# Keeping the first weights of all sixteen experts on chip, and picking a tile's weight there by a register address

## The chip, the cores and the metric

The kernel runs on one core of a Trainium2 chip. The core has a matrix engine (TensorE, PE in the rows, with a queue of its own for loading weights, PEld), a vector engine (VectorE, DVE), a scalar engine (ScalarE, ACT), GpSimd (POOL) and SyncE (SP), which here only issues DMAs. Each engine runs its own program in order, and they wait for one another by semaphores. SBUF is the memory on chip, PSUM (the `bank`s) the one that TensorE writes. The metric is the device time of one execution in microseconds (us); the number that counts is the median of three runs.

## The reference, cut to what matters

```python
patches = X.reshape(B, C, 8, 28, 8, 28).transpose(0, 2, 4, 1, 3, 5).reshape(B, 64, 2352)
h = concat([cls, einsum('bpi,hi->bph', patches, W) + b]) * pos_embed      # 128 images, 65 tokens, 128 wide
h = h + attention(layernorm(h))                                           # sliding window
x = layernorm(h); z = layer_norm(x, ln_in_g, ln_in_b)
gate = softmax((z @ router_w + router_b) / 0.7)
vals, idx = top_k(gate, 2)                                                # 2 of 16 experts per token
eh = silu(einsum('bsd,edh->ebsh', z, ew1) + eb1)                          # ew1: 16 x 128 x 512
ey = einsum('ebsh,ehd->ebsd', eh, ew2) + eb2                              # ew2: 16 x 512 x 128
mix = sum over the token's two experts of vals * ey
moe = mix + 0.25 * (silu(z @ sw1 + sb1) @ sw2 + sb2)
out = h + x + moe + silu(layer_norm(moe, ff_ln_g, ff_ln_b) @ ff_w1 + ff_b1) @ ff_w2 + ff_b2
```

Everything is float32.

## The kernel before

It is written engine by engine: each engine has one hand-written program, the order of its work is the order of that text, and semaphores carry the waits.

**Stage 1** takes the 128 images in 16 groups of 8 (512 tokens), forms the patch products, attention and the gate, and scatters each token's row twice by GpSimd into `z_rows` in DRAM, where each expert has a section of its own. The images lie in two buffers, the halves of `region`, each `XCOLS` = 14336 columns. The patch weights `wp` and the re-laid pieces `xf` and `xlast` are tensors of their own. The shared expert (`sh_up`, `sh_down`) runs for twelve of seventeen groups in the last group's gaps and behind it.

**Stage 2** is 80 expert tiles of 256 rows: the first 16 are experts 0 to 15, a tile each, the other 64 are handed out by a table that VectorE computes (`ejc`: a tile's expert, `rowj`: its first row). Four tiles are written out, then loops run over four tiles in a turn. For tile j:

- SP reads `rowj` and `ejc` into registers and issues the loads of the rows (`zin`), of `ew1` (L506) and of `ew2` (L508), each into one of four buffers. The `ew2` load waits until tile j-4 has left TensorE (`down_done`).
- TensorE in step j runs the transposes of the rows of tile j+1 (`t_in`, L1615), the first layer of tile j (`up`, L1626) and the second of tile j-1 (`down`, L1637), in this order.
- ScalarE takes the transposed rows from PSUM (L788) and applies silu to `up`'s four blocks (L798).
- VectorE in step j runs `split_rows(j+1)` (L1274, L1275, L1279), `split_w1(j+2)` (L1223, L1225) and `rows_out(j-1)` (L1265, L1268). The first layer's operands are taken apart into a high and a low part in a format that TensorE multiplies in one pass. So `split_w1` makes a cast of the weight (L1223) and a subtraction (L1225), into one of two buffers that `up` of two tiles before must have left. `rows_out` reads the tile's expert into a register (L1259) and adds the bias row, whose address comes from that register, to `down`'s result.
- GpSimd scatters the result to `y_tok` (L916).

In every fourth tile SP also loads residual rows (L542), to which VectorE adds a bias (`fb2_rows`, L1305).

Between stage 1 and the loop SP zeroes the tails of the experts' sections: L412 loads four numbers at a time into registers, L419 issues the writes. Then it loads the weights of stage 3 (L534), two groups of `ht` (L475) and enters the loop (L541).

**Stage 3** gathers each token's two rows, mixes, normalises and runs the last two layers, bound by TensorE.

The buffers of stages 2 and 3 lie over the image buffers in `region`, in an order made by `carve`. Constants that the diff uses: `E` = 16 experts, `W` = 512 columns of one expert's first weight, `FIRST` = 4 tiles whose weights are loaded ahead of time, `GROUPS` = 16, `EXPERT_TILES` = 80, `EARLY` = 12.

Of the kernel before, what the change touches and what calls it, by code (L numbers as in the profile page):

```python
# [68 lines left out]
FILL, EARLY = 7, 12  # L69
SP_TAILS = 12  # L70
# [42 lines left out]
def build(nc, consts, x, tok_w, tok_b, cls_tok, pos, w_c, ln_g, ln_b, r_w, r_b, ew1, eb1, ew2, eb2,  # L113
          sw1, sb1, sw2, sb2, f_g, f_b, fw1, fb1, fw2, fb2, out):
    with ExitStack() as ctx:
# [30 lines left out]
        wp = sb("wp", [P, MAIN, D])  # L146
# [13 lines left out]
        region = sb("region", [P, 2 * XCOLS])  # L160
# [7 lines left out]
        def carve(n):  # L168
            carved[0] += n
            assert carved[0] <= 2 * XCOLS  # L170
            return region[:, carved[0] - n:carved[0]]
# [9 lines left out]
        eh_at = carved[0]  # L181
        ehT = [carve(EC * EROWS).rearrange("p (c r) -> p c r", c=EC) for _ in range(2)]
        zin = [carve(EH * ZW).rearrange("p (h d) -> p h d", h=EH) for _ in range(4)]
        h2T = [carve(EROWS) for _ in range(2)]
        yout = [carve(EH * D).rearrange("p (h d) -> p h d", h=EH) for _ in range(2)]
        fw1_t = carve(DH)
        fw2_t = carve(EC * D).rearrange("p (c d) -> p c d", c=EC)
        r_at = carved[0]
        r_res = carve(TILES * D)
        HT_LOW = (XCOLS - r_at) // GTOK  # L190
        sh_res = carve(TILES * D)


        carved[0] = shared_with_stage3
# [4 lines left out]
        assert carved[0] <= eh_at  # L199
        carved[0] = eh_at  # L200
        gat = [carve(GT * TOPK * D).rearrange("p (t k d) -> p t k d", t=GT, k=TOPK) for _ in range(2)]
        assert 2 * GT * TOPK * D <= 2 * EC * EROWS + 4 * EH * ZW + 2 * EROWS + 2 * EH * D
# [6 lines left out]
        xf = sb("xf", [P, QUADS * 4 * HTOK])  # L209
        xquad = [xf[:, u * 4 * HTOK:(u + 1) * 4 * HTOK].rearrange("p (q t j) -> p q t j", q=2, j=2) for u in range(QUADS)]  # L210
        xlast = sb("xlast", [P, HTOK])
        eb2_rows = xf[:, 0:E * D]
        shs = [xf[:, E * D + u * SC * GTOK:E * D + (u + 1) * SC * GTOK].rearrange("p (c r) -> p c r", c=SC) for u in range(2)]
# [117 lines left out]
        w1_loaded = [sem(f"w1_loaded{u}") for u in range(4)]  # L331
# [94 lines left out]
        def _(sp):  # L426
# [67 lines left out]
            for i in range(HT_LOW, EARLY):  # L494
                load_ht(i)
# [445 lines left out]
        def _(dve):  # L941
# [354 lines left out]
            for j in range(4):  # L1296
                step2(j, j)
# [437 lines left out]
```

## Time and profile before

| | |
|---|---|
| runs | 907.56, 907.61, 908.23 us; median 907.61 us |
| profiled execution, from its first to its last instruction | 972.0 us |
| instructions in it | 22164 |
| busy of that span | TensorE 92%, VectorE 70%, ScalarE 62%, GpSimd 45% |
| read from and written to DRAM | 150.5 MB and 36.0 MB |
| stage 2, first to last `down` | 521.8 to 829.2 us |

The rows below come from that one execution. A time of a row counts from the start of its span. The span is longer than the median of the runs, which were made without a profile. A row of a group of instructions says how often, how long in all and in the mean, and how long the engine stood idle just before them, by what ended that. The end of a product on TensorE is modelled; starts are better to go by.

### The profile page before, as it was taken

To read this page: it belongs to the slowest core of one execution; us is meant where nothing else is said; L and a number is where in the kernel's file an instruction comes from. 1 tells how busy PE (TensorE), PEld (TensorE's weight loads), DVE (VectorE), ACT (ScalarE), POOL (GpSimd) and SP (SyncE) were. 2 spreads that over 40 slices of the span, in tenths; PEclk is the share of its full clock that TensorE was granted. 3 is DMA by queue.
4 is the path that set the end of the run, shared out by engine and by line. 5 is a ranking of instruction groups with operands and counts; after the bars stand their busy time and mean duration, and the time that the engine had idled before them with its cause. 6 is when DMAs were issued, how large, how long until landed. Compare 5 with 4: busy or idle time off the path is not lost. (4 is left out here: it accounts for less than half of the span.)

```text
span 972.0 us, 22164 instructions
## 1 busy us (share of the span) xinstructions
PE 896.2 (92%) x5920; PEld 801.2 (82%) x5920; DVE 676.2 (70%) x2244; ACT 599.5 (62%) x1064; POOL 438.8 (45%) x374
## 2 busy tenths in 40 slices
PE   2999999989999999999889999999999899789999
PEld 2788888778878888888779889898999899679888
DVE  8377877757877887787556666666676675488884
ACT  3567666656666666777645565555555565477766
POOL 6012554425555545554451445455555464334342
PEclk9999999979999999999879999999999999989999
DMA  9999999977788888767137687777778675334432
GB/s 225 224 221 225 242 247 240 237 205 210 213 228 218 214 216 219 194 216 213 50 105 215 196 227 218 214 219 228 216 224 236 184 221 166 107 82 115 107 103 57
DMA packets 194299, 186.96 MB, mean 192 GB/s; under 512 B 16797, under 2 KB 168698, under 8 KB 194010
## 3 DMA queue, kind: packets, MB, share of 16 engines
q1 hardware_dynamic: 183168, 166.24, 65.2%
q0 software_dynamic: 9376, 19.42, 6.1%
q10 hardware_dynamic: 1722, 0.93, 0.5%
q8 instruction: 12, 0.20, 0.1%
q14 instruction: 21, 0.17, 0.1%
HBM read 150.48 MB, written 36.04 MB: 192 GB/s over the span
## 5 line engine op out<-in xcount | busy, mean ns | idle before, releaser
L1435 PE MATMUL bank<-xf,wp 128*128 128x256 f32 x1280 | 314.0, 394 | 8.4 <-ACT xf L632 5.4
L1435 PEld LDWEIGHTS bank<-xf,wp 128*128 128x128 f32 x1280 | 237.7, 192 | 51.6 <-issue 7.4
L916 POOL DMA_INDIRECT y_tok<-region,dsti x160 | 162.9, 1018 | 164.9 <-DVE region L1268 119.0
L874 POOL TENSOR_TENSOR rstd<-var,neghalf 128x4 f32<-128x4 f32 (+2 forms) x51 | 80.6, 1580 | 287.9 <-DVE var L1030 156.4
L632 ACT ACTIVATE xf<-region 128x1024 f32<-128x1024 f32 x160 | 174.0, 1137 | 18.3 <-DVE region L947 18.3
L890 POOL DMA_INDIRECT z_rows<-z,posg x130 | 157.3, 1210 | 52.5 <-issue 52.2
L798 ACT ACTIVATE region<-bank,cols 128x256 f32<-128x256 f32 x320 | 132.3, 476 | 55.2 <-PE bank L1626 37.2
L1637 PE MATMUL bank<-region 128*128 128x128 f32 x1280 | 156.8, 275 | 1.1 <-DVE region L1268 1.0
L1637 PEld LDWEIGHTS bank<-region 128*128 128x128 f32 x1280 | 150.4, 192 | 1.7 <-issue 1.5
L1626 PE MATMUL bank<-parts 128*128 128x256 f32 x960 | 136.6, 290 | 14.2 <-DVE parts L1279 8.8
L1626 PEld LDWEIGHTS bank<-parts 128*128 128x128 f32 x960 | 119.6, 190 | 25.7 <-issue 19.0
L947 DVE COPY region<-region 32x1792 f32<-32x1792 f32 x96 | 104.8, 1092 | 50.3 <-ACT hT L652 28.9
L788 ACT ACTIVATE region<-bank,cols 128x256 f32<-128x256 f32 x80 | 45.4, 567 | 81.0 <-PE bank L1615 46.5
L1223 DVE CAST parts<-region 128x512 fp32r<-128x512 f32 x80 | 35.4, 443 | 70.9 <-DMA region<-in_L_ffn_ew 56.7
L1684 PE MATMUL bank<-region 128*128 128x128 f32 x520 | 61.7, 277 | 0.0
L1684 PEld LDWEIGHTS bank<-region 128*128 128x128 f32 x520 | 59.4, 192 | 0.9 <-ACT region L819 0.5
L1225 DVE TENSOR_TENSOR parts<-region,parts 128x512 fp32r<-128x512 f32 x80 | 55.6, 694 | 2.8
L1329 DVE SCALAR_TENSOR_TENSOR region<-region,w_all 128x128 f32<-128x128 f32 x130 | 50.3, 446 | 7.6 <-issue 5.3
L1665 PE MATMUL bank<-parts,wparts 128*128 128x512 f32 (+1 forms) x204 | 51.5, 403 | 3.4 <-DVE parts L1368 3.4
L1665 PEld LDWEIGHTS bank<-parts,wparts 128*128 128x128 f32 x204 | 37.5, 195 | 12.0 <-issue 3.6
L834 ACT ACTIVATE region<-region,nmr,rstd 128x128 f32<-128x128 f32 x65 | 26.9, 484 | 30.3 <-DVE nmr L1363 30.3
L819 ACT ACTIVATE region<-bank,cols 128x512 f32<-128x512 f32 (+1 forms) x68 | 40.6, 657 | 3.0 <-PE bank L1665 3.0
(183 smaller groups left out, 1232.3 us busy)
## 6 DMA issues: line engine op xcount, KB each, us to landing
region<-in_x SPq DMA_DIRECT2D x384, 196.0 KB
region<-in_L_ffn_ew SPq DMA_DIRECT2D x160, 256.0 KB
region<-z_rows SPq DMA_DIRECT2D x80, 130.0 KB
region<-y_tok SPq DMA_DIRECT2D x16, 512.0 KB, 3.6
ht_dram<-hT SPq DMA_DIRECT2D x16, 256.0 KB
r_dram<-rr SPq DMA_DIRECT2D x16, 256.0 KB
region<-ht_dram SPq DMA_DIRECT2D x16, 256.0 KB, 5.5
region<-r_dram SPq DMA_DIRECT2D x16, 256.0 KB
```

The source lines that it names most:

```text
L632: ins = act.activation(xquad[i].rearrange("p q t j -> p t q j"), src[:, :, 4 * i:4 * i + 4].rearrange("p t (q j) -> p t q j", j=2), ACT.Copy)
L798: act.activation(ehT[n % 2][:, c], bank[1 + c][:, 0:EROWS], ACT.Silu, bias=bias[c])\
L874: pool.tensor_tensor(dst, var, neghalf[:, 0:var.shape[1]], ALU.pow).then_inc(ready, 1)
L890: pool.indirect_dma_start(z_rows, bass.IndirectOffsetOnAxis(posg[k][:, n:n + 1], 0), z[k][:, t], None).then_inc(z_free[k], 16)
L916: pool.indirect_dma_start(y_tok, bass.IndirectOffsetOnAxis(dsti[n % 2][:, i:i + 1], 0), yout[n % 2][:, i], None).then_inc(y_free[n % 2], 16)
L947: dve.tensor_copy(dst, src).then_inc(block_moved, 1)
L1225: dve.tensor_tensor(w1l[n % 2], w1b[n % 4], w1h[n % 2], ALU.subtract).then_inc(w1l_ready, 1)
L1435: ins = pe.matmul(out_cols, wp[:, s], cols_in, start=s == 0, stop=s == MAIN - 1)
L1626: ins = pe.matmul(bank[1 + c][:, 0:EROWS], w[n % 2][:, c * P:(c + 1) * P], v[n % 2], start=i == 0, stop=i == len(terms) - 1)
L1637: ins = pe.matmul(bank[5 + n % 2][:, i * P:(i + 1) * P], ehT[n % 2][:, c, i * P:(i + 1) * P], w2b[n % 4][:, c], start=c == 0, stop=c == EC ...
L1665: ins = pe.matmul(dst, w[:, c * P:(c + 1) * P], v[:, 0:nt * P], start=i == 0, stop=i == len(terms) - 1)
L1684: ins = pe.matmul(bank[FFD_BANK[k]][:, t * P:(t + 1) * P], ffs[:, c, t * P:(t + 1) * P], fw2_t[:, c], start=c == 0 and t == 0, stop=c == E ...
```

## The change

The first weights of all 16 experts get one place each in a buffer `w1all` of 16 x 512 columns and are loaded once: four of them early in the last groups of stage 1 as before, four more (up to `W1_LOW` = 8) somewhat later, and experts 8 to 15 after the tails are zeroed, since their place is part of the second image buffer and of what follows it. In stage 2 SP loads only rows and second weights. VectorE's cast and subtraction read `w1all` at an address from a register. For that it loads the experts of seven tiles at once at the head of every four (`experts`, `four`), for the splits of tiles j+2 to j+5 and the bias rows of tiles j-1 to j+2; `rows_out` has no load of its own any more. The buffers are laid out anew in one larger `region`, which takes in what were `wp`, `xf` and `xlast`; `fw1_t` and `fw2_t` become tensors of their own. The first four `ew2` loads are issued later, behind group 14's stores.

```diff
-        region = sb("region", [P, 2 * XCOLS])
+        XF, XL, WP = QUADS * 4 * HTOK, HTOK, MAIN * D
+        ARENA = 2 * XCOLS + XF + XL + WP
+        region = sb("region", [P, ARENA])
...
+        r_res = carve(TILES * D)
         assert carved[0] <= XCOLS
-        shared_with_stage3 = carved[0]
-        w1b = [carve(W) for _ in range(4)]
+        w1_at = carved[0]
+        w1all = carve(E * W)
+        W1_LOW = (XCOLS - w1_at) // W
...
-            for i in range(HT_LOW):
+            def load_w1(e, done):
+
+                sp.dma_start(w1all[:, e * W:(e + 1) * W], ew1[e]).then_inc(done, 16)
+
+            for i in range(FIRST_HT):
                 load_ht(i)
-            for j in range(FIRST):
-                sp.dma_start(w1b[j], ew1[j]).then_inc(w1_loaded[j], 16)
-                sp.dma_start(w2b[j], ew2[j].rearrange("(c p) d -> p c d", p=P)).then_inc(w2_loaded[j], 16)
+            for e in range(FIRST):
+                load_w1(e, w1_loaded[e])
             one(stores, GROUPS - 3)
...
+            for i in range(FIRST_HT, EARLY):
+                load_ht(i)
+            for e in range(FIRST, W1_LOW):
+                load_w1(e, w1_low)
+            one(stores, GROUPS - 2)
             sp.wait_ge(xact_ready, units_before(GROUPS, 0))
-            for i in range(HT_LOW, EARLY):
-                load_ht(i)
-            one(stores, GROUPS - 2)
+            for j in range(4):
+                sp.dma_start(w2b[j], ew2[j].rearrange("(c p) d -> p c d", p=P)).then_inc(w2_loaded[j], 16)
...
                 ex = sp.value_load(ejc[0:1, bass.ds(j, 1)], min_val=0, max_val=E - 1)
-                sp.wait_ge(w1l_ready, j - 3)
-                sp.dma_start(w1b[n % 4], ew1[bass.ds(ex, 1)].rearrange("o d h -> d (o h)")).then_inc(w1_loaded[n % 4], 16)
                 sp.wait_ge(down_done, j - 3)
...
             zero_tails(sp, FIRST, SP_TAILS)
+            for e in range(W1_LOW, E):
+                load_w1(e, w1_high)
...
-            def split_w1(j, n, h):
+            def experts(j, n):
+
+                return nc.values_load_multi_w_load_instructions(ejc[0:1, bass.ds(j, n)], engines=[dve.engine],
+                                                                min_val=0, max_val=E - 1)[1]
+
+            def split_w1(j, n, ex):
 
                 dve.wait_ge(up_done, j * EC - EC) if n > 1 else None
-                dve.wait_ge(w1_loaded[n % 4], h * 16 + 16)
-                dve.tensor_copy(w1h[n % 2], w1b[n % 4]).then_inc(w1h_ready, 1)
+                w1 = w1all[:, bass.ds(ex * W, W)]
+                dve.tensor_copy(w1h[n % 2], w1).then_inc(w1h_ready, 1)
                 dve.wait_ge(w1h_ready, j + 1)
-                dve.tensor_tensor(w1l[n % 2], w1b[n % 4], w1h[n % 2], ALU.subtract).then_inc(w1l_ready, 1)
+                dve.tensor_tensor(w1l[n % 2], w1, w1h[n % 2], ALU.subtract).then_inc(w1l_ready, 1)
...
-            def rows_out(j, n, h_):
-
-                ex = dve.value_load(ejc[0:1, bass.ds(j, 1)], min_val=0, max_val=E - 1)
+            def rows_out(j, n, h_, ex):
+
...
+            def four(j, n, q=0, after=None):
+
+                ex = experts(j - 1, 7)
+                for m in range(4):
+                    step2(j + m, n + m, q, ex[m + 3], ex[m])
+                    if after and m == 0:
+                        after()
...
+            dve.wait_ge(w1_loaded[3], 16)
+            step2(1, 1, 0, 3, 0)
+            dve.wait_ge(w1_low, 16 * (W1_LOW - FIRST))
+            step2(2, 2, 0, 4, 1)
+            step2(3, 3, 0, 5, 2)
+            dve.wait_ge(w1_high, 16 * (E - W1_LOW))
             dve.wait_ge(w3_loaded, 48)
...
             with dve.Fori(1, 1 + GROUPS) as i:
-                for n in range(4):
-                    step2(i * 4 + n, 4 + n, i - 1)
-                    if n == 0:
-                        fb2_rows(i - 1)
+                four(i * 4, 4, i - 1, lambda: fb2_rows(i - 1))
```

In SP's program at the passage to stage 2, the rows of before run from the last tail (L419) over the weights of stage 3 (`ffn_ff_w`), two `ht` loads and the loop's head to the residual load (`r_dram`):

```order
L419 DMA z_rows<-zeros 128x260
L534 DMA region<-in_L_ffn_ff_w 128x512
L534 DMA region<-in_L_ffn_ff_w 128x4x128
L534 DMA fbq<-in_L_ffn_ff_b 128x128
L475 DMA region<-ht_dram 128x512 x2
L541 UNCONDITIONAL_BRANCH
```

The same place after:

```order
L421 DMA z_rows<-zeros 128x260
L486 DMA region<-in_L_ffn_ew 128x512 x8
L543 DMA fw_t<-in_L_ffn_ff_w 128x512
L543 DMA fw_t<-in_L_ffn_ff_w 128x4x128
L543 DMA fbq<-in_L_ffn_ff_b 128x128
L477 DMA region<-ht_dram 128x512 x2
L550 UNCONDITIONAL_BRANCH
```

Eight loads of first weights now stand ahead of the stage-3 weights and of everything that the loop issues.

In VectorE's program at the head of its stage-2 loop, before (ISA are register and wait instructions; CAST is L1223 on the weight and L1274 on the rows):

```order
L1274 CAST parts<-region 128x256
L1275 ISA
L1275 SCALAR_TENSOR_TENSOR dstf<-region,ejb 128x2
L1279 TENSOR_TENSOR parts<-region,parts 128x256
L1221 ISA
L1222 ISA
L1223 CAST parts<-region 128x512
L1224 REGISTER_ALU
L1225 TENSOR_TENSOR parts<-region,parts 128x512
L1259 ISA
L1259 TENSOR_LOAD ejc
L1259 ISA x2
```

And after:

```order
L1230 TENSOR_LOAD ejc
L1230 ISA x14
L1286 ISA
L1287 REGISTER_ALU
L1288 CAST parts<-region 128x256
L1289 ISA
L1289 SCALAR_TENSOR_TENSOR dstf<-region,ejb 128x2
L1293 TENSOR_TENSOR parts<-region,parts 128x256
L1235 ISA
L1237 ISA
L1237 COPY parts<-region 128x512
L1238 REGISTER_ALU
```

The register load, with two instructions for each of seven numbers, moved from the middle of each tile to the head of four, ahead of `split_rows`, and the wait for the weight's load (L1222) is gone. The weight's cast stands as COPY because its source's address is not fixed in the program.

## Rows read from the trace of the kernel before

**Rows 1.** Table by stretches: start:end, length, busy time by engine, clock, DMA share, GB/s.

```profile
0.00:23.00 23.00, 4.71 (x22) 4.58 (x23) 19.21 (x29) 7.27 (x12) 16.37 (x16) 0.97 0.93 225
...
540.00:820.00 280.00, 262.64 (x2157) 249.17 (x2156) 181.34 (x519) 160.20 (x378) 145.62 (x144) 1.00 0.76 217
...
sum 972.00, PE 896.20 PEld 801.21 DVE 676.20 ACT 599.48 POOL 438.79; mean PE 149.37 PEld 133.54 DVE 112.70 ACT 99.91 POOL 73.13
```

**Rows 2.** TensorE in order of time at stage 2's start: start, length, line, operation.

```profile
525.39 1.95 PE L1637 MATMUL bank<-region 128*128 128x128 f32 x16
527.18 0.40 PE L1615 MATMUL bank<-cst,region 128*128 128x128 f32 x2
...
528.84 1.95 PE L1637 MATMUL bank<-region 128*128 128x128 f32 x16
```

**Rows 3.** Line 1637 (`down`): count, shortest/median/longest in ns, first and last start.

```profile
L1637 PEld LDWEIGHTS bank<-region x1280: 186/192/192, 521.8 to 829.2; 128*128 128x128 f32 x183
```

**Rows 4.** VectorE's groups from 540 to 820: busy us, mean ns, idle before.

```profile
L1225 DVE TENSOR_TENSOR parts<-region,parts 128x512 fp32r<-128x512 f32 x72 | 50.0, 695 | 2.5
L1223 DVE CAST parts<-region 128x512 fp32r<-128x512 f32 x71 | 31.6, 445 | 67.7 <-DMA region<-in_L_ffn_ew 53.6 <-PE bank L1626 13.9
...
L1305 DVE TENSOR_TENSOR region<-region,fbq 128x512 f32 (+1 forms) x16 | 10.5, 656 | 0.0
```

**Rows 5.** SP's waits from 540 to 820: us in total, times, longest.

```profile
SPq L508 <- remote: 2.0, 3, 1.6
```

**Rows 6.** SP's issues in order of time at stage 2's start.

```profile
519.24 0.89 SPq L534 DMA_DIRECT2D region<-in_L_ffn_ff_w  x2
...
523.51 0.37 SPq L514 DMA_DIRECT2D region<-z_rows  x1
524.72 0.35 SPq L506 DMA_DIRECT2D region<-in_L_ffn_ew  x1
525.17 0.40 SPq L508 DMA_DIRECT2D region<-in_L_ffn_ew  x1
526.62 0.68 SPq L514 DMA_DIRECT2D region<-z_rows  x1
```

**Rows 7.** SP's register load of a tile's expert, and its weight load; columns as rows 3.

```profile
L504 SPq TENSOR_LOAD <-ejc x76: 3/274/684, 524.0 to 815.9; - x76
...
L506 SPq DMA_DIRECT2D region<-in_L_ffn_ew x76: 4/318/725, 524.7 to 816.6; - x76
```

**Rows 8.** VectorE in order of time, 600 to 605.5.

```profile
601.10 0.29 DVE L1274 CAST parts<-region 128x256 fp32r<-128x256 f32 x1
...
601.44 0.44 DVE L1279 TENSOR_TENSOR parts<-region,parts 128x256 fp32r<-128x256 f32 x1
...
603.27 0.16 DVE L1265 TENSOR_TENSOR dsti<-dstf,cst 128x2 uint32<-128x2 f32 x1 [0.33 <-issue]
```

**Rows 9.** Register loads: VectorE's of one number, SP's of four; columns as rows 3.

```profile
L1259 DVEq FUSED_REGOPS  x112: 53/190/210, 523.3 to 828.8; - x112
L1259 DVEq TENSOR_LOAD <-ejc x80: 300/308/658, 522.7 to 828.5; - x80
L1259 DVEq SEQ_ASSERT  x80: 23/23/41, 523.6 to 829.1; - x80
...
L412 SPq TENSOR_LOAD <-tail x3: 309/378/511, 497.1 to 515.7; - x3
```

**Rows 10.** Stretches with loads of 2 KB lines; columns as rows 1.

```profile
426.00:429.00 3.00, 3.00 (x15) 2.51 (x14) 1.63 (x10) 3.00 (x4) 1.04 (x1) 1.00 1.03 385
...
520.00:527.00 7.00, 7.00 (x63) 6.94 (x62) 4.64 (x14) 5.09 (x13) 1.36 (x2) 1.00 0.91 255
```

**Rows 11.** A stand of TensorE late in stage 1 and the stretch behind it.

```profile
469.20:472.60 3.40, 0.30 (x3) 0.11 (x1) 0.69 (x1) 2.38 (x5) 1.08 (x2) 0.96 0.12 39
472.40:479.10 6.70, 6.40 (x27) 6.21 (x28) 2.31 (x20) 4.38 (x10) 0.00 (x0) 0.50 0.23 83
```

More of the change, by code:

```diff
@@ L69 @@
 FILL, EARLY = 7, 12
+FIRST_HT = 6
 SP_TAILS = 12
@@ L207, in build @@
         h2h, h2l = ([parts[:, 4 * W + (2 * c + u) * EROWS:4 * W + (2 * c + u + 1) * EROWS] for u in range(2)] for c in range(2))
[L209 removed]
+        xf = region[:, 2 * XCOLS:2 * XCOLS + XF]
         xquad = [xf[:, u * 4 * HTOK:(u + 1) * 4 * HTOK].rearrange("p (q t j) -> p q t j", q=2, j=2) for u in range(QUADS)]
[L211 to L213 removed]
+        xlast = region[:, 2 * XCOLS + XF:2 * XCOLS + XF + XL]
+        wp = region[:, 2 * XCOLS + XF + XL:ARENA].rearrange("p (s h) -> p s h", s=MAIN)
         wparts = sb("wparts", [P, 2 * DH + 2 * DS], F32R)
@@ L330, in build @@
         tail_ready, ejb_done, ejt_ready, tej_done = sem("tail_ready"), sem("ejb_done"), sem("ejt_ready"), sem("tej_done")
-        w1_loaded = [sem(f"w1_loaded{u}") for u in range(4)]
+        w1_loaded = [sem(f"w1_loaded{u}") for u in range(FIRST)]
+        w1_low, w1_high = sem("w1_low"), sem("w1_high")
         w2_loaded = [sem(f"w2_loaded{u}") for u in range(4)]
@@ L1285, in step2 @@
                     split_rows(j + 1, n + 1)
-                if not static or j + 2 < EXPERT_TILES:
-                    split_w1(j + 2, n + 2, q + (n + 2) // 4)
-                if n >= 1 and not (static and j > EXPERT_TILES):
-                    rows_out(j - 1, n - 1, q * 2 + (n - 1) // 2)
+                if ex_in is not None:
+                    split_w1(j + 2, n + 2, ex_in)
+                if ex_out is not None:
+                    rows_out(j - 1, n - 1, q * 2 + (n - 1) // 2, ex_out)
+            def four(j, n, q=0, after=None):
[4 more added lines that the diff above has]
+                        after()
             sh_rows(EARLY - 1)
@@ L1293, in _ @@
             split_rows(0, 0)
-            split_w1(1, 1, 0)
+            dve.wait_ge(w1_loaded[1], 16)
+            split_w1(1, 1, 1)
             dve.wait_ge(eb2_loaded, 16)
-            for j in range(4):
-                step2(j, j)
+            dve.wait_ge(w1_loaded[2], 16)
+            step2(0, 0, 0, 2)
+            dve.wait_ge(w1_loaded[3], 16)
[4 more added lines that the diff above has]
+            dve.wait_ge(w1_high, 16 * (E - W1_LOW))
             dve.wait_ge(w3_loaded, 48)
@@ L1307, in _ @@
             with dve.Fori(1, 1 + GROUPS) as i:
-                for n in range(4):
-                    step2(i * 4 + n, 4 + n, i - 1)
-                    if n == 0:
-                        fb2_rows(i - 1)
+                four(i * 4, 4, i - 1, lambda: fb2_rows(i - 1))
             for i in range(1 + GROUPS, EXPERT_TILES // 4 - 1):
-                for n in range(4):
-                    step2(i * 4 + n, i * 4 + n)
+                four(i * 4, i * 4)
             fb2_rows(GROUPS, 1)
-            for j in range(EXPERT_TILES - 4, EXPERT_TILES):
-                step2(j, j)
+            ex = experts(EXPERT_TILES - 5, 5)
+            for m in range(4):
+                step2(EXPERT_TILES - 4 + m, EXPERT_TILES - 4 + m, 0, ex[m + 3] if m < 2 else None, ex[m])
             dve.wait_ge(up_done, EXPERT_TILES * EC)
```

30 lines of the change are left out of this document (14 added, 16 removed).

## The prediction, made before the changed kernel ran

> **What bounds the kernel now.** I read the table by stretches first. In the 280 us from 540 to 820, the expert tiles (stage 2), TensorE is busy for 262.6 us, VectorE for 181.3 and the others for less, and the DMA engines for 76% [rows 1]. So TensorE has most of the work, and the question is what holds it up. At the stage's start, where every tile's weights are already on chip, its order of a tile (two transposes of tile j+1, twelve products of `up(j)`, sixteen of `down(j-1)`) comes round every 3.45 us: `down` at 525.39 and at 528.84 [rows 2]. Over the whole stage 80 `down` take from 521.8 to 829.2, 3.87 us a tile for 79 steps (307.4/79) [rows 3]. The difference, 0.42 x 79 = 33 us, is all that a change which leaves TensorE's work as it is can win there.
>
> VectorE's groups in the same stretch show a wait: the cast of the first weight, L1223, stood idle 67.7 us, 53.6 of them for the load of `ew1` [rows 4]. Why the load is late is seen on SP. Its longest entry of waiting in these 280 us is 2.0 us in all [rows 5]: it is not stopped by buffers that are not free, it is itself at its limit, and issues the loads as fast as it can. From one row load to the next it needs 3.11 us (523.51 to 526.62) [rows 6], and every fourth tile has a loop's turn and a residual load besides.
>
> But SP's rows hold a warning. A register load from `ejc` has a median of 274 ns, a least of 3 and a most of 684 [rows 7]. A read cannot take 3 ns: such records are written in a bunch after a stop. I infer that the taking of the trace stops SP, and that part of the 3.87 us is the profile's own. The totals say the same. The span is 972.0 us and the median of the runs 907.61, 64.4 less. TensorE is busy 896.2 us of the span and idle 75.8, of which 18.3 lie in the first 23 us, before its main work [rows 1]. If its work is not shorter without a profile, only 907.6 - 896.2 = 11.4 us of idle can be left in a timed run, 15% of the 75.8 (less still if a run's time holds anything around the span). So most of the 33 us is not there to be won.
>
> **The change part by part.** *The load per tile goes.* SP loses 76 weight loads, 0.32 us median each [rows 7], some 0.45 us from its start to that of the next (524.72 to 525.17) [rows 6]. SP then needs 2.7 us a tile and no longer sets the pace; VectorE's 53.6 us go with it. What is late next is TensorE itself, at 3.45 us. Gain: 33 us in the profile's own time. In a timed run I take 15% of it, 5 us, by the share of idle that can be left; bounds are 0 (nothing left there) and 33 (all of it real).
>
> *The split by a register address.* Cast and subtraction keep their size, 445 and 695 ns [rows 4]. The trace has no one-source copy at an address from a register; the two-source addition at such an address, L1305, takes 656 ns, no more than the static subtraction of its size, 695. So I take 445, the nearest row; the upper bound is the two-source rate, 695, as if the copy lost its double rate. The Trainium skill (Vector Engine (DVE) Microarchitecture Reference, 5.1 Performance modes) names only type, place and shape as conditions of the double rate, not how the address came; by that the cost is nothing, but no row here shows it.
>
> *The register loads move into a lump.* Before, each tile loads one number, and the engine stands idle about 0.33 us for it (603.27) [rows 8]. Now seven are loaded at the head of four tiles. By rows the load takes 0.31 us, and the clamp and check of each number 0.19 + 0.02 [rows 9], with gaps about 0.28: 0.31 + 7 x 0.28 = 2.3 us once, against 4 x 0.33. VectorE is busy 181.3 us in 280 [rows 1], 2.5 us for each tile of 3.87; four tiles and the lump are 10.0 + 2.3 = 12.3, against TensorE's 13.8, so as a sum it fits. Queued behind the lump is `split_rows`, for which `up` waits. The lump starts when `down(j-1)` ends and the addition behind it is sent off: some 0.3 us, 2.3 of loads and 0.8 for `split_rows` (601.10 to 601.88) [rows 8] are 3.4 us. `up(j+2)` starts one tile, 3.45 us, and the transposes after that `down` ends: just in time. I book 1 us over the 19 lumps, between 0 and 5. A load of four registers takes 378 ns here, against 274 to 308 for one [rows 7, 9], so the count hardly matters. The Trainium skill (Runtime: NRT & Kernel Launch, Instruction fetch mechanics) says otherwise of loads from HBM: some 200 ns for each register even in bulk; by that seven would take about 1.4 us (an estimate) and the lump 3.4.
>
> *Eight weights enter SP's queue at the start of stage 2.* Experts 8 to 15, 256 KB each and 2.1 MB together, are issued behind the zeroing of tails and ahead of the stage-3 weights, two `ht` loads, the residual load and the rows of tile 4. Everything behind them lands later by their transfer. The DMA engines moved 385 GB/s in the best stretch of such loads and 255 in the mixed one just here [rows 10]: 5.4 to 8.2 us. I take 6. The rows of tile 4 are issued at 523.51 and TensorE takes them at 527.18 with no wait [rows 2, 6]. At 3.67 us from issue to use, and with 1.3 MB queued ahead since 519.2, there is little slack; I take 0.5 (0 to 1.5). TensorE's order is fixed: behind the transposes of tile 4 stand `up(3)` and `down(2)`, so it stands still 5.5 us. After a stand of 3.2 us at 469 the granted clock fell to half, 0.50 from 472.4 to 479.1 [rows 11]; the same here costs half of 6.7, 3.4 us (0 to 5). Sum: 8.9 us, from 4 (385 GB/s, most slack, no fall) to 13.
>
> *Other moves cost nothing.* The first four `w2` loads and experts 4 to 7 move within a stretch before 475 us, 40 us ahead of their first use; without that cover they would cost what the eight above do. The new layout adds no instruction. The early tiles' wait for `w1(4)` ends; by rows 2 the tiles there ran at full pace, so nothing is won.
>
> **Sum.** In the profile's own time: 972.0 - 33 + 8.9 + 1 = 948.9. In a timed run: 907.6 - 5 + 8.9 + 1 = 912.5.
>
> **Rivals.** *The wait is in the timed runs too (faster).* Place: SP's queue in every tile. For it: SP hardly waits, and 3.11 us and its share of the loop's turn is close to 3.45, so a little slowness lets it set the pace. Against it: the 11.4 us. Half to all of the 33 us gained, less 9.9: 907.6 - 16.5 + 9.9 = 901.0 down to 884.5; I give it 893. It decides the sign from 10 us of real waiting on.
>
> *No stand at the start (faster, a little).* If the rows of tile 4 have 6 us of slack without a profile, 907.6 - 5 + 1 = 903.6. Against it: TensorE reaches that place with little waiting in its way [rows 2].
>
> *The parts cancel.* Between the forecast and these, 907.6.
>
> *VectorE becomes the bound (slower still).* The copy at 695 adds 0.25 us a tile, or the load of seven goes by the slowest load of four, 511 ns ((511 - 274)/3 = 79 ns for each further register, 0.5 us a lump [rows 7, 9]). Either uses up the margin of 0.1 us behind each lump and pushes `up` back by 0.2 to 0.5 us in 18 lumps of seven, both together by 0.7: 4 to 13 us on top of the forecast, 916 to 925. Against it: the median load of four took only 70 ns longer than VectorE's load of one. By the Trainium skill's 200 ns for each register (Runtime: NRT & Kernel Launch) it would be 1.1 us a lump and some 932 us.
>
> **How the numbers follow.** Forecast 0.42 (its own range 909.5 to 918), wait real 0.28, no stand 0.08, cancel 0.14, VectorE 0.08. Within 0.2%, 1.8 us, is what a measurement of this kernel can hardly tell from no change. So faster 0.36, same 0.14, slower 0.50. The range must reach into the first rival and stop short of the last: 892 leaves out about a tenth, 919 another.
>
> **What would show it.** Right: TensorE idle 4 to 7 us before the transposes of tile 4 with the `z_rows` load as releaser, a clock near 0.5 behind it, L1223's wait for `ew1` gone, SP waiting for `down`, and a tile at 3.45 to 3.55 us in the loop. Wrong: no idle there; a timed run below 903, which would mean that SP held up the timed runs as well; or `up` waiting for `split_rows` at every fourth tile for more than 0.3 us. The forecast rests most on the 11.4 us: if TensorE's own work is shorter without a profile, more idle is left than that, and more can be won.

## The result and the profile after

The changed kernel takes 953.84 us (median; 950.55 to 956.1) against 907.92 for the kernel before on the same chip: ratio 1.0506, 95% interval 1.0483 to 1.053. It is slower by 46 us. The direction was the one forecast; the size was not, 912.5 with a range to 919.

Two places hold nearly all of it. The first rows are TensorE's longest waits after, over the whole run (us in total, times, longest):

```profile
PE bank L1652 <- DVE parts L1293: 31.3, 19, 2.4
...
PE bank L1641 <- DMA region<-z_rows: 7.4, 1, 7.4
```

L1652 is `up`, L1293 the subtraction in `split_rows`: one of the signs that the prediction had named as proving it wrong. L1641 are the transposes of a tile, here of tile 4. Next, VectorE and TensorE in order of time around one head of four tiles (start, length, line, operation; in brackets the idle time before it and who ended it), and the register work of line 1230, which loads the expert numbers (shortest, median, longest in ns; first and last start):

```profile
547.16 0.42 DVE L1282 TENSOR_TENSOR region<-bank,region 128x256 f32<-128x256 f32 x1 [0.56 <-PE bank L1663]
551.45 0.29 DVE L1288 CAST parts<-region 128x256 fp32r<-128x256 f32 x1 [3.87 <-ACT region L797]
...
551.80 0.42 DVE L1293 TENSOR_TENSOR parts<-region,parts 128x256 fp32r<-128x256 f32 x1
```

```profile
550.28 0.38 PE L1641 MATMUL bank<-cst,region 128*128 128x128 f32 x2
552.35 1.70 PE L1652 MATMUL bank<-parts 128*128 128x256 f32 x12 [1.69 <-DVE parts L1293]
```

```profile
L1230 DVEq FUSED_REGOPS  x131: 183/183/210, 516.3 to 801.9; - x131
L1230 DVEq SEQ_ASSERT  x131: 23/23/41, 516.6 to 802.1; - x131
L1230 DVEq TENSOR_LOAD <-ejc x19: 1186/1702/1889, 514.4 to 799.5; - x19
```

VectorE does nothing that counts as busy from 547.58 to 551.45. The row blames ScalarE (L797), but what lies in the 3.87 us is the lump: the load at 1.70 us, where the prediction had 0.31, then seven comparisons and checks of 183 + 23 ns with gaps, 0.275 us each. It is 3.63 us, not 2.3. `up` starts 2.07 us after the transposes before it; in the other tiles it is 0.14. So a tile that takes 3.43 us takes 5.4 at a head. By the rows of waits that is 31 of the 46 us. Those rows count from the modelled end of the product before; by the starts, the delays at the 19 heads add up to 36.

The stand at the stage's start is the other place. TensorE at tile 4, and a table by stretches (columns as rows 1):

```profile
506.94 0.69 PE L1641 MATMUL bank<-cst,region 128*128 128x128 f32 x2 [7.42 <-DMA region<-z_rows]
507.27 2.91 PE L1652 MATMUL bank<-parts 128*128 128x256 f32 x12
```

```profile
499.20:506.90 7.70, 0.32 (x3) 0.13 (x2) 0.42 (x1) 0.00 (x0) 2.48 (x3) 0.73 1.00 340
502.70:512.90 10.20, 5.96 (x28) 5.97 (x29) 1.95 (x6) 2.55 (x6) 0.34 (x1) 0.50 0.52 170
540.00:800.00 260.00, 233.19 (x1990) 229.50 (x1989) 160.96 (x480) 143.03 (x347) 134.46 (x133) 0.99 0.51 147
```

TensorE stands 7.4 us while the DMA engines are full (1.00, 340 GB/s), and works the next 6 us at clock 0.50, the lower of its two levels (1.2 GHz), at which twelve `up` products last 2.91 us instead of 1.67. In the loop the DMA share has fallen from 0.76 [rows 1] (0.84 in c1 below) to 0.51: the load per tile is really gone. VectorE's and SP's rows of the same stretch show the rest of what was forecast, the cast by a register address (L1237), and SP waiting for `down` where it hardly waited before [rows 5]:

```profile
L1237 DVE CAST parts<-region 128x512 fp32r x66 | 28.0, 425 | 4.2
```

```profile
SPq L515 <- PE bank L1663: 81.3, 67, 4.2
```

### The profile page after: what moved, and what is told of

Its sections match the earlier page's. It is cut to its first block and busy times, and to the rows that moved or that the text cites. A ratio compares the mean times of both kernels' runs of the same rounds, so it can differ in the third digit from the quotient of the medians.

```text
span 954.0 us, 22010 instructions
## 1 busy us (share of the span) xinstructions
PE 875.2 (92%) x5920; PEld 793.6 (83%) x5920; DVE 669.5 (70%) x2244; ACT 595.8 (62%) x1064; POOL 437.0 (46%) x374
## 5 line engine op out<-in xcount | busy, mean ns | idle before, releaser
L1461 PE MATMUL bank<-region 128*128 128x256 f32 x1344 | 323.3, 391 | 7.0 <-ACT region L641 7.0
L1461 PEld LDWEIGHTS bank<-region 128*128 128x128 f32 x1344 | 247.1, 190 | 53.2 <-issue 4.6
L641 ACT ACTIVATE region<-region 128x1024 f32<-128x1024 f32 x160 | 173.8, 1135 | 22.7 <-DVE region L956 22.7
L1652 PE MATMUL bank<-parts 128*128 128x256 f32 x960 | 137.3, 293 | 31.3 <-DVE parts L1293 31.3
L1663 PE MATMUL bank<-region 128*128 128x128 f32 x1280 | 158.5, 278 | 0.0
L807 ACT ACTIVATE region<-bank,cols 128x256 f32<-128x256 f32 x320 | 126.6, 475 | 50.2 <-PE bank L1652 49.8
L1663 PEld LDWEIGHTS bank<-region 128*128 128x128 f32 x1280 | 153.0, 195 | 0.0
L1652 PEld LDWEIGHTS bank<-parts 128*128 128x128 f32 x960 | 122.1, 194 | 36.0 <-issue 35.1
L797 ACT ACTIVATE region<-bank,cols 128x256 f32<-128x256 f32 x80 | 45.2, 565 | 102.2 <-PE bank L1641 101.0
L1288 DVE CAST parts<-region 128x256 fp32r<-128x256 f32 x80 | 23.4, 292 | 91.8 <-ACT region L797 81.2
L1710 PE MATMUL bank<-fw_t,region 128*128 128x128 f32 x520 | 61.7, 277 | 0.0
L1710 PEld LDWEIGHTS bank<-fw_t,region 128*128 128x128 f32 x520 | 59.4, 192 | 1.0 <-ACT region L828 0.5
L1282 DVE TENSOR_TENSOR region<-bank,region 128x256 f32<-128x256 f32 x80 | 33.8, 422 | 19.7 <-PE bank L1663 19.1
```

The costliest lines, as they stand in the source:

```text
L641: ins = act.activation(xquad[i].rearrange("p q t j -> p t q j"), src[:, :, 4 * i:4 * i + 4].rearrange("p t (q j) -> p t q j", j=2), ACT.Copy)
L807: act.activation(ehT[n % 2][:, c], bank[1 + c][:, 0:EROWS], ACT.Silu, bias=bias[c])\
L1461: ins = pe.matmul(out_cols, wp[:, s], cols_in, start=s == 0, stop=s == MAIN - 1)
L1652: ins = pe.matmul(bank[1 + c][:, 0:EROWS], w[n % 2][:, c * P:(c + 1) * P], v[n % 2], start=i == 0, stop=i == len(terms) - 1)
L1663: ins = pe.matmul(bank[5 + n % 2][:, i * P:(i + 1) * P], ehT[n % 2][:, c, i * P:(i + 1) * P], w2b[n % 4][:, c], start=c == 0, stop=c == EC ...
L1710: ins = pe.matmul(bank[FFD_BANK[k]][:, t * P:(t + 1) * P], ffs[:, c, t * P:(t + 1) * P], fw2_t[:, c], start=c == 0 and t == 0, stop=c == E ...
```

## The experiments

All ratios are to the kernel before, run on the same chip in between.

| kernel | ratio | 95% interval | median us |
|---|---|---|---|
| changed | 1.0506 | 1.0483 to 1.053 | 953.84 |
| a1, single registers | 1.0084 | 1.006 to 1.0109 | 914.88 |
| a2, weights earlier | 1.0426 | 1.04 to 1.0452 | 945.76 |
| a3, both | 1.002 | 1.0008 to 1.0033 | 909.43 |
| b1, before with the lump | 1.0432 | 1.0404 to 1.0459 | 946.18 |
| c2, a2 without checks of numbers | 1.0024 | 1.0008 to 1.004 | 911.06 |
| c3, a2 with five, twice | 1.0295 | 1.0264 to 1.0325 | 934.78 |
| c4, a3 with seven on SP | 1.0347 | 1.0313 to 1.038 | 938.5 |
| f1, a2 with the list one further | 1.0285 | 1.0232 to 1.0337 | 933.2 |
| d1, rows first | 0.9988 | 0.9974 to 1.0002 | 906.23 (905.76 without one run of 2255, which the ratio leaves out) |

### Which part costs what: a1, a2, a3, b1

a1 takes the lump away and nothing else; VectorE reads one number at a time:

```diff
-                return nc.values_load_multi_w_load_instructions(ejc[0:1, bass.ds(j, n)], engines=[dve.engine],
-                                                                min_val=0, max_val=E - 1)[1]
+                return dve.value_load(ejc[0:1, bass.ds(j, 1)], min_val=0, max_val=E - 1)
...
-                ex = experts(j - 1, 7)
                 for m in range(4):
-                    step2(j + m, n + m, q, ex[m + 3], ex[m])
+                    step2(j + m, n + m, q, True, True)
...
-                    split_w1(j + 2, n + 2, ex_in)
+                    split_w1(j + 2, n + 2, experts(j + 2, 1) if ex_in is True else ex_in)
...
-                    rows_out(j - 1, n - 1, q * 2 + (n - 1) // 2, ex_out)
+                    rows_out(j - 1, n - 1, q * 2 + (n - 1) // 2, experts(j - 1, 1) if ex_out is True else ex_out)
```

> The changed kernel, but VectorE reads the expert numbers one register at a time: one load ahead of each weight split, one ahead of each rows_out, two a tile, eight in four tiles instead of one load of seven. All else is as changed. Theory: the 46 us lost are 18 lumps of 1.85 us of TensorE's waiting (33 us; the load of seven takes 1.70 us where one register takes 0.31, and its checks 1.9 us, all of it ahead of split_rows) and the stand of 7.4 us ahead of tile 4 with some 3.4 us of half clock behind it. With the lump gone 907.9 + 7.4 + 3.4 = 918.7 us (915 to 922). Rival A, it is the sum of VectorE's register work that counts: eight loads with their checks are 8 x 0.58 = 4.7 us in four tiles, more than the lump's 3.6, so 954 or above. Rival B, the new layout of the buffers or the addressed read slows the loop, wherever the loads stand: about 950.

Measured: 914.88, 0.1 us under the range. Of TensorE's waits from 490 to 760 us one is left, the stand at tile 4:

```profile
PE bank L1638 <- DMA region<-z_rows: 8.2, 1, 8.2
```

Eight loads and their checks in four tiles are more register work than the lump (0.31 + 0.275 us each), and TensorE does not wait for VectorE in the whole loop; each interruption is shorter than the slack where it stands. Rivals A and B fall.

a2 moves the eight loads of experts 8 to 15 in SP's queue:

```diff
             for j in range(4):
                 sp.dma_start(w2b[j], ew2[j].rearrange("(c p) d -> p c d", p=P)).then_inc(w2_loaded[j], 16)
+            for e in range(W1_LOW, E):
+                load_w1(e, w1_high)
...
             zero_tails(sp, FIRST, SP_TAILS)
-            for e in range(W1_LOW, E):
-                load_w1(e, w1_high)
```

> The changed kernel, but the eight loads of experts 8 to 15 stand in SP's queue right behind the four loads of second weights, some 30 us earlier, and no longer ahead of the rows of tile 4. Theory: the stand of 7.4 us ahead of the transposes of tile 4 goes, and the half clock of 3.4 us behind it: 953.8 - 10.8 = 943 us (940 to 947). Rival A, the time is taken elsewhere, since the same 2.1 MB move beside the stores of z rows that tile 0 waits for, and stage 2 begins later: 951 to 955. Rival B, the stand comes from the last loads of stage 2's start whatever stands in the queue (final weights, stage-one rows): 953.8, with a wait of 5 us or more still there.

Measured: 945.76, 8.1 us less than the changed kernel (7.3 by the two ratios). Of the 7.4 us of standing 2.3 are still there, as the rows below show.

a3 has both edits.

> Both edits: single registers, and the eight loads earlier. Theory: the two parts are the whole loss and add up, 953.8 - 35 - 10.8 = 908 us (904 to 911), the time of the kernel before, since its timed loop stood on TensorE's floor of 3.45 us a tile and had nothing for shorter queues to give. Rival A, the loop of before did wait for SP and its loads in timed runs too: 0.2 to 0.4 us a tile come back, 876 to 892. Rival B, something else in the layout costs: 915 to 945.

Measured: 909.43. The rows are TensorE's waits between 490 and 810 us in a2 and then, to 510, in a3, and a3's loop:

```profile
PE bank L1652 <- DVE parts L1293: 31.6, 19, 2.7
PE bank L1641 <- DMA region<-z_rows: 2.3, 1, 2.3
```

```profile
PE bank L1638 <- DMA region<-z_rows: 2.2, 1, 2.2
```

```profile
540.00:760.00 220.00, 220.00 (x1924) 220.00 (x1924) 165.30 (x465) 138.17 (x336) 131.47 (x129) 1.00 0.57 168
```

In a3 TensorE has no idle time at all in 220 us of the loop, a tile every 3.433 us, and the kernel is within 0.2% of the kernel before. So the lump and the stand are nearly the whole loss: 8.1 (changed to a2), 36.3 (a2 to a3) and 1.6 left over against before, more than nothing by a3's interval, which no run here explains.

b1 puts the lump alone into the kernel before, whose weights are still loaded for each tile:

```diff
             with dve.Fori(1, 1 + GROUPS) as i:
+                ex = experts(i * 4 - 1, 7)
                 for n in range(4):
-                    step2(i * 4 + n, 4 + n, i - 1)
+                    step2(i * 4 + n, 4 + n, i - 1, ex[n])
```

> The kernel before, first weights still loaded for each tile, with one thing of the change: VectorE loads seven expert numbers in one instruction at the head of four tiles (four of them are used, for the rows of the second bias) instead of one at each tile. Theory: the lump alone costs 1.7 to 1.85 us of TensorE's waiting at each of 18 heads: 907.9 + 31 to 33 = 940 us (935 to 945). Rival A, the lump hides in the slack ahead of split_rows as the prediction had it (1 us in all): 908 to 911. Rival B, its price shows only together with the weights that are addressed by it: 908.

Measured: 946.18, 1.2 us over the range given. The lump's price needs neither the weights on chip nor the new layout. `up` waits there 31.2 us in all:

```profile
PE bank L1634 <- DVE parts L1285: 31.2, 18, 3.1
```

The time lost to the lump is 36 to 39 us in the three pairs (changed to a1, a2 to a3, before to b1), more than these rows of 31 us. By the starts of TensorE's products the delays at the heads of a2 add up to 36. Behind the longest of its waits, 2.68 us where the usual one is 1.69, the granted clock falls to its lower level (1.2 GHz) as well, for 3.4 us (columns as rows 1):

```profile
731.80:735.20 3.40, 3.40 (x19) 3.40 (x18) 2.87 (x10) 1.72 (x4) 1.78 (x2) 0.51 0.22 74
```

### What the kernel before really does: c1

The same kernel before, profiled once more.

> The kernel before, unchanged, profiled once more. Theory: its 972.0 us in the profile shown ahead are 64 us more than its runs take, and that excess belongs to that one capture: with a capture like those of the changed kernels (span 2 us under the time) the span is 906 us, stage 2 lasts 280 us (3.5 us a tile, TensorE's floor with the half clock in it), and VectorE's waits for first weights of 12.5 us in the loop and SP's full queue are gone or under 2 us. Rival: the span is again some 970 us with 3.87 us a tile, so that the wait was there in every profiled execution.

Its span is 909.1 us (the run took 910.94) where the profile shown ahead has 972.0. Its loop (columns as rows 1), then VectorE's cast of the weight (as rows 4), SP's waits from 540 to 760 and SP's register load (as rows 5 and 7):

```profile
540.00:760.00 220.00, 218.68 (x1910) 218.34 (x1909) 160.63 (x461) 136.77 (x333) 129.22 (x129) 1.00 0.84 244
```

```profile
L1223 DVE CAST parts<-region 128x512 fp32r<-128x512 f32 x63 | 28.0, 445 | 29.8 <-DMA region<-in_L_ffn_ew 29.1 <-issue 0.3
```

```profile
SPq L508 <- PE bank L1637: 14.3, 34, 1.1
```

```profile
L504 SPq TENSOR_LOAD <-ejc x76: 270/278/436, 496.6 to 756.8; - x76
```

TensorE is idle 1.3 us of 220, and all tiles there but two take 3.43 us; in the first profile it was 17.4 of 280 [rows 1]. The least register load is 270 ns and not 3 [rows 7]. So the 3.87 us a tile [rows 3] were that one capture's, as the prediction inferred from the totals. One part of the theory falls: the wait of L1223 for its weight, which I had expected to vanish, is still 29.1 us. It belongs to a VectorE that has time to spare, and TensorE beside it is busy for 99.4%. It never was a sign of anything to win.

### How much the lump may last: c2, c3

c2 is a2 with the comparison and check of each number left out, which the trace has at 0.275 us:

```diff
                 return nc.values_load_multi_w_load_instructions(ejc[0:1, bass.ds(j, n)], engines=[dve.engine],
-                                                                min_val=0, max_val=E - 1)[1]
+                                                                min_val=0, max_val=E - 1,
+                                                                skip_runtime_bounds_check_because="ejc holds expert numbers, cut off at E - 1")[1]
```

> The changed kernel with the weights earlier (945.8 us), its load of seven registers as it is, but without the comparison and check of each number behind it (seven times 0.275 us by the trace). Theory: in that kernel a lump of 1.70 + 7 x 0.275 = 3.63 us makes TensorE wait 1.85 us, so 1.78 us of it lie in slack; the load alone, 1.70 us, then fits in and TensorE waits 0 to 0.2 us: 910 us (907 to 914), the time of the kernel with single loads. Rival A, it is the load itself that holds things up (its data come late, whatever follows): 941 to 946. Rival B, the wait shrinks in proportion: 909.4 + 36.4 x 1.70 / 3.63 = 926 us.

Measured: 911.06, from 945.76. The load is as long as before, and TensorE waits for `split_rows` three times in the whole stage:

```profile
L1230 DVEq TENSOR_LOAD <-ejc x19: 1187/1707/1882, 508.3 to 757.0; - x19
```

```profile
PE bank L1652 <- DVE parts L1293: 1.8, 3, 0.7
```

So the slack ahead of `split_rows` at the loop's head holds about 1.7 us, and each further 0.1 us of lump is 0.1 us of TensorE, at the 18 heads of seven (at the last, of five, `up` is late by 0.3 only). A cost that starts at a threshold is why rival B's proportion fails.

c3 has two loads of five in four tiles:

```diff
-                ex = experts(j - 1, 7)
                 for m in range(4):
-                    step2(j + m, n + m, q, ex[m + 3], ex[m])
+                    if m % 2 == 0:
+                        ex = experts(j + m - 1, 5)
+                    step2(j + m, n + m, q, ex[m % 2 + 3], ex[m % 2])
```

> The changed kernel with the weights earlier (945.8 us), with a load of five registers at the head of every second tile instead of one of seven at the head of four. Theory, a fixed slack per lump: the lump is 1.19 + 5 x 0.275 = 2.57 us, 0.79 us over the slack of 1.78, at 36 places: 909.4 + 28 = 938 us (932 to 943), with a wait of 0.7 to 0.9 us at each. Rival A, register work counts by its sum (ten registers for seven): 909.4 + 36.4 x 2 x 2.57 / 3.63 = 961 us. Rival B, five fit into the slack and nothing is left: 910 us.

Measured: 934.78, inside the range, but not with the waits that were expected. TensorE in order of time, one place in mid-loop and one at the loop's head:

```profile
545.70 0.38 PE L1642 MATMUL bank<-cst,region 128*128 128x128 f32 x2
546.26 1.70 PE L1653 MATMUL bank<-parts 128*128 128x256 f32 x12 [0.18 <-DVE parts L1293]
...
549.58 0.38 PE L1642 MATMUL bank<-cst,region 128*128 128x128 f32 x2
549.72 1.67 PE L1653 MATMUL bank<-parts 128*128 128x256 f32 x12
...
553.01 0.38 PE L1642 MATMUL bank<-cst,region 128*128 128x128 f32 x2
554.14 1.70 PE L1653 MATMUL bank<-parts 128*128 128x256 f32 x12 [0.74 <-DVE parts L1293]
```

From transposes to `up` it is 0.14 us undisturbed, 0.56 in mid-loop and 1.13 at the head: `up` is late by 0.42 and 0.99, 1.41 us in four tiles, and 18 times that is 25, which is the time measured over a3. The lump is 2.58 us at the first place and 2.70 at the second (there its load takes 1.31 us), so the slack is 2.2 us in mid-loop and 1.7 at the head, where the loop's turn (0.4 us between the sending of L1282 and the load in the changed kernel) comes ahead of it. The changed kernel has a head without that turn, the second of the two fours that are written out behind the loop:

```profile
787.45 0.38 PE L1641 MATMUL bank<-cst,region 128*128 128x128 f32 x2
788.96 1.70 PE L1652 MATMUL bank<-parts 128*128 128x256 f32 x12 [1.12 <-DVE parts L1293]
```

There `up` is late by 1.37 us, against 1.93 at a head in the loop; the lump is 3.57 us, so the slack is again 2.2.

### What a load of registers costs: c4, e1, e2, f1

The prediction took the price from a load of four on SP, 378 ns [rows 9]. Two things could set it apart from VectorE's seven: the engine, or the count. c4 adds a load of seven, used for nothing, to SP's loop in a3:

```diff
             with sp.Fori(1, 1 + GROUPS) as i:
+                nc.values_load_multi_w_load_instructions(ejc[0:1, bass.ds(i * 4 - 1, 7)], engines=[sp.engine],
+                                                         min_val=0, max_val=E - 1)
```

> The kernel with single registers and the weights earlier (909.4 us), with a load of seven registers on SP at each of the 16 heads of its loop, used for nothing. It prices the disputed step on the engine from which the prediction took it (four registers in 378 ns on SP). Theory: the price is of VectorE, SP's load takes 0.3 to 0.6 us. Rival: the price is of the count, 1.2 us or more on any engine. The time: SP waits for TensorE's down products in nearly every tile, so 909.4 us (907 to 912) either way; 912 or more if SP has less slack than its waits show.

Measured: 1.48 us for the load, so the engine is not it; and 938.5 us, against the 909.4 of both theories. What came is the expectation's last words, that SP has less slack than its waits show. SP's load, TensorE's waits and SP's own, 495 to 760 us:

```profile
L551 SPq TENSOR_LOAD <-ejc x16: 1467/1478/1646, 495.9 to 729.9; - x16
```

```profile
PE bank L1640 <- DMA region<-z_rows: 25.3, 16, 1.9
```

```profile
SPq L517 <- PE bank L1662: 21.1, 28, 1.1
```

SP still waits for `down` 28 times and yet makes TensorE wait at each of its 16 heads, for the rows that it sends too late. Its lump is 1.48 + 7 x 0.25 = 3.2 us, TensorE's wait 1.6 in the mean, or 1.8 by the time ((938.5 - 909.43)/16): the slack of an engine that waits 56 us in a3 from 495 to 760 is about 1.5 us at one place. A sum of waits says nothing about how long a single interruption may be.

e1 and e2 measure the load itself, at the end of the programs of VectorE and SP in a3:

```diff
+            for _ in range(2):
+                for at, n in ((16, 1), (16, 2), (16, 4), (16, 5), (16, 7), (16, 8),
+                              (19, 1), (19, 2), (19, 4), (19, 5), (19, 7), (19, 8)):
+                    nc.values_load_multi_w_load_instructions(ejc[0:1, at:at + n], engines=[sp.engine],
+                                                             min_val=0, max_val=E - 1)
```

> The disputed cost by itself: the kernel with single registers and the weights earlier, and at the very end of VectorE's and of SP's program 24 loads each of 1, 2, 4, 5, 7 and 8 registers, used for nothing, once from element 16 of the list and once from element 19. Known so far: VectorE 1 at 0.31, 5 at 1.19, 7 at 1.70 us; SP 1 at 0.28, 4 at 0.31 to 0.38, 7 at 1.47 us; the four stood at a multiple of four, the five and the seven one ahead of it. Theory A, it is the count and each register over the first costs 0.2 to 0.25 us: 4 take 0.9 to 1.0 us at either place, 8 take 1.7 to 1.95. Theory B, it is the place: loads from a multiple of four take 0.3 to 0.5 us whatever the count up to 8, and from one ahead of it 0.2 us and more a register. Theory C, up to four are one fetch at either place (0.3 to 0.4) and 5 to 8 take 1.2 us and more at either place. The time itself says nothing: the loads lengthen the end by some 20 us.

e1 gave no price: its loads had no use and no check, and are not in its trace. It is a3 once more (906.49 us, one run).

> The loads of the run before (1, 2, 4, 5, 7 and 8 registers, from element 16 and from element 19 of the list, on VectorE and on SP, at the end of their programs), with the check of each number kept, since loads with neither a use nor a check were left out of the program by the compiler. Theory A, count: each register over the first costs 0.2 to 0.25 us, so 4 take 0.9 to 1.0 us and 8 take 1.7 to 1.95 at either place. Theory B, place: from element 16 0.3 to 0.5 us whatever the count, from element 19 0.2 us and more a register. Theory C, fetches of up to four: 1, 2 and 4 take 0.3 to 0.4 us at either place, 5, 7 and 8 take 1.2 us and more. The time itself says nothing.

e2 (957.58 us in one run, with the loads at its end) has them. Four of SP's loads in e2, the second time round, each picked from the trace by its stretch: seven and eight registers from element 16, then seven and eight from element 19:

```profile
L603 SPq TENSOR_LOAD <-ejc x1: 929/929/929, 934.0 to 934.0; - x1
```

```profile
L603 SPq TENSOR_LOAD <-ejc x1: 532/532/532, 936.7 to 936.7; - x1
```

```profile
L603 SPq TENSOR_LOAD <-ejc x1: 1468/1468/1468, 945.1 to 945.1; - x1
```

```profile
L603 SPq TENSOR_LOAD <-ejc x1: 1665/1665/1665, 948.3 to 948.3; - x1
```

All of them, in ns, the second time round (the first agrees within 33 ns but for VectorE's first load, 502):

| registers | 1 | 2 | 4 | 5 | 7 | 8 |
|---|---|---|---|---|---|---|
| SP, from element 16 | 274 | 481 | 309 | 534 | 929 | 532 |
| SP, from element 19 | 269 | 474 | 862 | 1066 | 1468 | 1665 |
| VectorE, from element 16 | 318 | 545 | 350 | 615 | 1042 | 604 |
| VectorE, from element 19 | 312 | 536 | 962 | 1178 | 1625 | 1841 |

None of the three theories has it whole; B is nearest. From a multiple of four elements a full four costs about what one costs, and each register left over 0.2 us: on SP four take 309 where one takes 274, and eight take 532 where two take 481. From element 19 every register costs 0.2 us singly, even where a full four lies within (20 to 23). c3's fives, which start one ahead of a multiple at the loop's head and one behind it in mid-loop, take 1.31 and 1.19 us at the places shown; loads from two behind a multiple are in no run. The Trainium skill (Runtime: NRT & Kernel Launch, Instruction fetch mechanics) has some 200 ns for each register even in bulk, of loads from HBM; the lower rows agree, (1468 - 269)/6 = 200 on SP, the upper do not. The load of four behind the prediction's price [rows 9] starts at a multiple of four, the changed kernel's seven start one ahead of it (`j - 1`).

f1 tries this in the loop: a2, with the list lying one element further on in memory, so that `j - 1` falls on a multiple of four.

```diff
-        ejc = sb("ejc", [1, EXPERT_TILES], I32)
+        ejc = sb("ejc", [1, EXPERT_TILES + 1], I32)[:, 1:]
```

> The changed kernel with the weights earlier (945.8 us), with the same loads of seven registers and the same checks, but the list of expert numbers lies one element further on in its memory, so that the seven start at a multiple of four elements. Theory, from the prices measured at the end of the program (seven on VectorE: 1.04 us from such a place, 1.63 from one ahead of it): the load in the loop falls from 1.70 to some 1.1 us, TensorE's wait at each of 18 heads from 1.85 to some 1.25 us, and the time to 945.8 - 11 = 935 us (932 to 938). Rival A, the place counts only where the address is fixed, not where a register gives it as in this loop: 944 to 948. Rival B, the wait hangs on something else that the load's length merely goes with: 944 to 948 with a load of 1.1 us.

Measured: 933.2, 12.6 us less than a2 for a shift of four bytes. The load falls by 0.6 us and TensorE's wait by 11.1 in all. The lump is 1.11 + 1.93 = 3.0 us, and by the starts `up` is late by 1.3 at a head of the loop: again 1.7 us of slack.

```profile
L1230 DVEq TENSOR_LOAD <-ejc x19: 592/1106/1322, 505.5 to 778.3; - x19
```

```profile
PE bank L1652 <- DVE parts L1293: 20.5, 19, 1.8
```

### A version against both: d1

d1 is a3 with the rows of tile 4 first in SP's queue. The three loads of final weights go behind the expert weights (their tiles have a place of their own in the new layout), two `ht` loads behind the loop, and in the loop the residual load goes behind the first tile's loads:

```diff
-            for dst, src in ((fw1_t, fw1), (fw2_t, fw2.rearrange("(c p) d -> p c d", p=P)),
-                             (fbq[:, :], fb2.partition_broadcast(P))):
-                sp.dma_start(dst, src).then_inc(w3_loaded, 16)
-            load_ht(EARLY)
-            load_ht(EARLY + 1)
...
             with sp.Fori(1, 1 + GROUPS) as i:
+                expert_loads(i * 4, 4)
                 sp.dma_start(r_res[:, bass.ds(i * GTOK - GTOK, GTOK)].rearrange("p (t d) -> p t d", t=GT),
                              r_dram[:, bass.ds(i * GT - GT, GT)]).then_inc(r_loaded, 16)
-                for n in range(4):
+                for n in range(1, 4):
                     expert_loads(i * 4 + n, 4 + n)
```

> A version meant to beat both kernels: single registers and the weights earlier (909.4 us), and in SP's queue nothing but waits is left ahead of the rows of tile 4: the final weights, which the new layout lets in earlier, go behind the expert weights, two late loads behind the loop, and the first residual rows behind the rows. Theory: the 2.3 us for which TensorE still waits ahead of the transposes of tile 4, and some 1.5 us of half clock behind it, go: 906.5 us (904.5 to 908.5), 0.1 to 0.4 per cent under the kernel before. Rival A: the wait goes and the clock's fall stays for its other reasons: 907 to 909. Rival B: what is moved delays the rows of tiles 0 to 3 or the residual rows of the first group instead: 910 to 914.

Measured: 906.23, ratio 0.9988 with an interval that reaches to 1.0002. The transposes of tile 4 now start without a wait:

```profile
501.06 0.38 PE L1639 MATMUL bank<-cst,region 128*128 128x128 f32 x2
```

By the two ratios the kernel is some 0.3% under a3; against the kernel before it is no difference that these runs can tell from none.

## Why the prediction was wrong

**The bound: right.** The prediction set 33 us of apparent waiting against the totals and put nearly all of it down to the taking of the profile. c1 shows TensorE busy for 99.4% of the loop, and a tile in 3.46 us in the mean against 3.433 in a3: of the 5 us booked as a gain at most 0.027 x 79 = 2.1 were there. (307.4/79 is 3.89 and not 3.87, so the 33 us are 35 by that sum; no step hangs on it.) The reading of SP as at its limit [rows 5, 6] and of L1223's wait as its mark [rows 4] came from the same distorted capture and was wrong for the real runs, where SP waits 14.3 us for `down`.

**The split by a register address: right.** 425 ns against 445 before. The Trainium skill (Vector Engine (DVE) Microarchitecture Reference, 5.1 Performance modes), which does not count the address among its conditions, and this row agree.

**The lump: the step that failed.** Booked at 1 us (0 to 5), it costs 31 us in `up`'s waits, 36 by the starts, and 36 to 39 in time. Two numbers in it were wrong. "A load of four registers takes 378 ns here, against 274 to 308 for one [rows 7, 9], so the count hardly matters": the seven take 1.70 us, since they do not start where the four do (e2, f1). And "just in time" left 3.5 - 0.3 - 0.8 = 2.4 us for the lump: c2 and c3 put it at 1.7 at the loop's head. The loop's turn of 0.4 us stands there too, which was not in the sum, and from the lump's end (547.58 + 3.63 = 551.21) to `up` (552.35) it is 1.1 us and not 0.8. With the lump as booked, 2.27 us, the smaller slack alone would have cost 0.57 x 18 = 10 us; the load's price brings the other 1.36 x 18 = 24. The prediction's own words show what was missed: with a margin worked out at 0.1 us, every error in it counts eighteen times in full, and the range gave it 5 us.

**The stand at the stage's start: right in place, kind and size.** Booked 5.5 us of standing and 3.4 of half clock, 8.9 (4 to 13). The trace has 7.4, and 6 us of work at clock 0.50, some 3 us lost; moving the loads gave back 8.1 us with the lump (changed to a2) and 5.4 without it (a1 to a3). The kernel before has 2.1 us of this wait itself in c1, and the prediction's trace had none [rows 2]; so part of the 7.4 us is not the change's doing.

**The other moves at nothing: nearly right.** a3 has them all and stands 0.2% over before (0.08 to 0.33%).

**The rivals.** That the wait was in the timed runs is refuted by c1, and by a3, which removes SP's load per tile and wins nothing. VectorE as the bound was the mechanism that came, but its condition was too mild: 79 ns for a further register, 916 to 925. The figure of 932 that stood beside it, with 200 ns for each, had the load nearly right (1.4 estimated, 1.7 measured) and the slack wrong.

## What to carry to other kernels

Price a moved step by a row of the same form: here a register load took a full four from a multiple of four elements at about the price of one, and 0.2 us for each register from elsewhere, so align the list or load one at a time. An engine's total of idle time does not tell what one interruption costs; add up the chain at the place, with the loop's turn and the register work that no busy time shows, from what releases the engine to what the bottleneck waits for. And where a span lies far above the runs, as 972 above 908, profile again before reading waits from it: a second capture here showed a kernel whose TensorE had nothing left to give.

## What the runs showed that was not expected

The price of a register load by where it starts: eight registers in 532 ns from element 16, 1665 from element 19. The slack of SP, at about 1.5 us in a place, while its waits add up to 56. And a single capture that stretched the way from the first `down` to the last from 277 us (c1) to 307 [rows 3], with register loads of 3 ns in it.
